# Token sums on VectorE, the first pair's rows by selection products, fillers among the gates, and a tail in permuted token order

## What is computed

```python
xn = layernorm(x)
# block 1: time mix (a scan over tokens, WKV) and channel mix
h = ln(xn); hp = shift(h); xk, xv, xr = mix(h, hp)
k, v, r = xk @ w_tk, xv @ w_tv, sigmoid(xr @ w_tr)
x1 = xn + r * wkv(time_decay, time_first, k, v)
h2 = ln(x1); x1 = x1 + sigmoid(cr @ w_cr) * (relu(ck @ w_ck) ** 2 @ w_cv)
# block 2: attention, 16 heads of 8 channels, weights = dense + gated low rank experts
pooled = xn.mean(axis=1)
gates, idx = softmax(top_k(relu(pooled @ gw1.T + gb1) @ gw2.T + gb2, 2))
q, k, v = svd_moe(xn, ...)            # per batch: Wm + sum of gated U S V
ctx = softmax(q @ k.T) @ v
out = x + x1 + svd_moe(ctx, ...)
```

## Time and profile before

| | |
|---|---|
| median of 3 runs | 487.45 us (486.83 to 490.58) |
| profiled execution | 487.07 us, span from first to last instruction 485.3 us |
| TensorE busy | 443.6 us, 91% |
| VectorE busy | 372.2 us, 77% |
| ScalarE busy | 354.2 us, 73% |
| POOL busy | 180.9 us, 37% |

### The profile page before, as it was taken

How to read it: one execution, slowest core, us unless ns; L and a number is a source line. 1 busy time by engine, 2 the same in 40 slices (tenths; PEclk the granted TensorE clock), 3 DMA queues, 4 the chain that set the end, 5 groups by cost and what they waited for, 6 DMA issues and landing times.

```text
span 485.3 us, 8374 instructions
## 1 busy us (share of the span) xinstructions
PE 443.6 (91%) x3156; PEld 147.9 (30%) x3158; DVE 372.2 (77%) x670; ACT 354.2 (73%) x453; POOL 180.9 (37%) x236
## 2 busy tenths in 40 slices
PE   2886998999999999999999999999999999989996
PEld 2751322222223322222232222222322222222275
DVE  7543997999988689999877899998778999940113
ACT  2266773689888666898986668989875689899651
POOL 7048940414651414146514141375141313751200
PEclk9999995999999999999999999999999999999998
DMA  6004421132323223323232232332322321102132
GB/s 219 11 8 52 61 23 23 12 54 26 57 22 59 19 45 33 51 28 56 23 58 22 28 51 50 30 52 26 57 24 22 55 45 12 28 9 80 31 105 91
DMA packets 46684, 21.35 MB, mean 44 GB/s; under 512 B 37556, under 2 KB 37684, under 8 KB 46644
## 3 DMA queue, kind: packets, MB, share of 16 engines
q1 hardware_dynamic: 45824, 20.13, 25.5%
q10 hardware_dynamic: 820, 0.68, 0.4%
HBM read 4.88 MB, written 5.24 MB: 21 GB/s over the span
## 4 chain that ended last, share of the span: by engine, by line
PE 58%; DVE 23%; ACT 13%; issue 2%; SPq 2%; DMA 1%; DVEq 0%
PE banks L1341 17%; DVE neg_half L1080 15%; PE banks L1330 12%; PE banks L1256 11%; ACT probs L887 9%; PE banks L1302 8%; DVE run L1038 3%; PE banks L1231 2%; PE banks L1164 2%; PE banks L1388 2%; PE banks L1383 2%; PE banks L1129 1%; ACT work L846 1%; SPq L431 1%; ACT work L844 1%
## 5 line engine op out<-in xcount | busy, mean ns | idle before, releaser
L1080 DVE TENSOR_REDUCE neg_half<-banks 128x1 f32<-128x512 f32 x512 | 319.1, 682 | 39.1 <-PE banks L1256 37.4
L887 ACT ACTIVATE probs<-banks 128x1024 f32<-128x1024 f32 x256 | 247.7, 1022 | 66.3 <-PE banks L1330 63.6
L1341 PE MATMUL banks<-probs,v_op 128*32 128x512 f32 x1024 | 137.2, 608 | 0.4 <-ACT probs L887 0.4
L1256 PE MATMUL banks<-k_main,q_main 64*128 64x512 bf16 x512 | 120.3, 388 | 15.0 <-DVE neg_half L1080 12.1
L1330 PE MATMUL banks<-q_main,k_main 64*128 64x512 bf16 x512 | 101.2, 382 | 5.0 <-ACT probs L887 3.7
L1330 PE MATMUL banks<-q_tail,k_tail 35*128 35x512 bf16 x512 | 100.9, 381 | 0.0
L1256 PEld LDWEIGHTS banks<-k_main,q_main 64*128 64x128 bf16 x512 | 36.0, 94 | 168.1 <-DVE neg_half L1080 145.2
L1330 PEld LDWEIGHTS banks<-q_main,k_main 64*128 64x128 bf16 x512 | 26.0, 95 | 44.5 <-ACT probs L887 32.1
L1330 PEld LDWEIGHTS banks<-q_tail,k_tail 35*128 35x128 bf16 x512 | 26.6, 95 | 23.7 <-issue 1.1
L1061 DVE TENSOR_TENSOR rec<-banks,quarter_in 128x512 f32<-128x512 f32 x4 | 2.8, 690 | 37.8 <-PE banks L1302 37.8
L700 POOL TENSOR_TENSOR work<-work 128x512 f32<-128x512 f32 x12 | 12.5, 1040 | 49.8 <-ACT work L872 49.8
(11 more groups left out here) (164 smaller groups left out, 429.4 us busy)
## 6 DMA issues: line engine op xcount, KB each, us to landing
ctx_dram<-ctx_sb SPq DMA_DIRECT2D x16, 256.0 KB, 2.0
q_main<-parts SPq DMA_DIRECT2D x64, 48.0 KB
k_main<-parts SPq DMA_DIRECT2D x64, 48.0 KB
parts<-ctx_dram SPq DMA_DIRECT2D x8, 256.0 KB, 4.4
mat_sb<-in_mats_dram SPq DMA_DIRECT2D x2, 768.0 KB, 5.3
q_tail<-max_parts SPq DMA_DIRECT2D x96, 2.0 KB
q_main<-parts SPq DMA_DIRECT2D x32, 32.0 KB
k_main<-parts SPq DMA_DIRECT2D x32, 32.0 KB
```

The costliest lines, as they stand in the source:

```text
L887: a.activation(probs[:, (2 * step + h) % 4, :, :], banks[:, 2 * h:2 * h + 2, :], ACT.Exp).then_inc(b_read, 1)
L1080: v.tensor_reduce(neg_half[:, s, u:u + 1], src, axis=AX.X, op=ALU.max, negate=True).then_inc(a_read, 1)
L1256: mm(dst, q_main[HALF * e:HALF * (e + 1), s, P * c:P * c + P], k_main[HALF * e:HALF * (e + 1), s, CHUNK * h:CHUNK * h + CHUNK], start=True ...
L1341: last = mm(banks[g:g + 32, PV_BANK, :], v_op[:, s % 2, step, e, :], probs[:, (2 * step + h) % 4, e, :], start=(step == 0), stop=(step == ...
```

## The change

1. Token sums: VectorE sums four tiles of a chunk (`sum_tiles`) into `xn_sum` once all tiles are normalised, and 4 products instead of 16 finish the sums. The transposes of x come before them.
2. The gate chain loses two steps (`chosen`, `gates`), and `warm(n)` issues n bf16 products of 128 columns into an unused bank: 4, 8, 32, 12 and 4 of them among the gate products.
3. Pair 0's rows: a selection matrix `row_of` (built by ScalarE in 22 small copies) times the parts gives `q_main` and `k_main` of pair 0, 12 products and 4 evictions. SyncE's `load_pair(0, 0)` is gone.
4. `turn_h`, the first `values_of` and `mix_product` move into the loop of places, by the table `FILL_JOBS` (place: jobs). ScalarE's order is as before, with two evictions of pair 0's rows ahead of `hT`.
5. `RT` and the last contexts (`ctx_out_T`) are written in permuted token order, so that the tail's weights are adjacent columns.
6. `k_tail` is set to 1.0 by one memset, and POOL adds the value bias in 4 instructions instead of 16.

```diff
+FILL_JOBS = {2: [("turn", 0), ("turn", 1)], 5: [("turn", 2), ("turn", 3)], 8: [("values", 0)], 11: [("values", 1)]}
+FILL_JOBS.update({14 + 2 * m: [("mixed", m)] for m in range(6)})
+FILL_JOBS.update({26: [("values", 2)], 28: [("values", 3)]})
+FILL_JOBS.update({29 + (m - 6): [("mixed", m)] for m in range(6, 12)})
+FILL_JOBS.update({35 + j: [("project", j, 1)] for j in range(4)})
+FILL_JOBS.update({39 + 4 * i + j: [("part", j, 1, i)] for i in range(2) for j in range(4)})
...
-            load_pair(0, 0)
             load_tails(0, 0)
...
-                for k in range(CHUNK // P):
-                    tc = 4 * (n % 2) + k
-                    here = V[:, 8 * (n // 2):8 * (n // 2) + 8, tc, :]
-                    last = g.tensor_tensor(here, here, vb_ob[:, 0:1, :].rearrange("p o (r w) -> p (o r) w", w=2 * HD),
-                                           ALU.add)
-                last.then_inc(v_ready, 1)
+                g.tensor_tensor(here, here, vb_ob[:, 0:1, :].rearrange("p o (r w) -> p r o w", w=2 * HD).to_broadcast(
+                    [P, 8, 4, 2 * HD]), ALU.add).then_inc(v_ready, 1)
...
+            act.wait_ge(rows_ps, 1)
+            a.copy(q_main[:, 0, 0:CHUNK], bank(0)).then_inc(q_rows_kept, 1)
+            act.wait_ge(rows_ps, 3)
+            a.copy(k_main[:, 0, CHUNK:], bank(3)).then_inc(k_rows_kept, 1)
...
+            def sum_tiles(n):
+
+                dve.wait_ge(xn_ready, 4 * n + 4)
+                v.tensor_reduce(xn_sum[:, n, :], xn_tok[:, 4 * n:4 * n + 4, :].rearrange("p k c -> p c k"), axis=AX.X,
+                                op=ALU.add).then_inc(xn_summed, 1)
...
+            for n in range(CHUNKS):
+                sum_tiles(n)
             dve.wait_ge(pooled_ps, B)
...
-            link(v.tensor_scalar(chosen[:, :], rank[:, :], 2.0, None, ALU.is_lt))
             dve.wait_ge(gexp_ready, 1)
-            link(v.tensor_tensor(gexp[:, :], gexp[:, :], chosen[:, :], ALU.mult))
+            link(v.scalar_tensor_tensor(gexp[:, :], rank[:, :], 2.0, gexp[:, :], ALU.is_lt, ALU.mult))
...
-            link(v.tensor_scalar(gates[:, :], gexp[:, :], gsum[:, 0:1], None, ALU.mult))
-            v.tensor_copy(gates_r[:, :, :], gates[:, :].rearrange("b (e o) -> b e o", o=1).to_broadcast(
-                [B, EXPERTS, RANK])).then_inc(gates_ready, 1)
+            v.tensor_scalar(gates_r[:, :, :], gexp[:, :].rearrange("b (e o) -> b e o", o=1).to_broadcast(
+                [B, EXPERTS, RANK]), gsum[:, 0:1], None, ALU.mult).then_inc(gates_ready, 1)
...
+            dve.wait_ge(rows_ps, 2)
+            v.tensor_copy(k_main[:, 0, 0:CHUNK], bank(2)).then_inc(k_rows_kept, 1)
+            dve.wait_ge(rows_ps, 4)
+            v.tensor_copy(q_main[:, 0, CHUNK:], bank(1)).then_inc(q_rows_kept, 1)
...
-                    v.tensor_tensor(RT[:, :, bass.ds(q * QT, QT)], x1[:, :, :], gx[:, :, :], ALU.add
-                    ).then_inc(rt_ready, 1)
+                    half, at = divmod(q, 2)
+                    there = RT[:, :, CHUNK * half:CHUNK * (half + 1)].rearrange("c b (k p) -> c b p k", k=CHUNK // P)
+                    there = there[:, :, QT // 4 * at:QT // 4 * (at + 1), :]
+                    for b in range(B):
+                        last = v.tensor_tensor(there[:, b, :, :], x1[:, b, :].rearrange("c (p k) -> c p k", k=CHUNK // P),
+                                               gx[:, b, :].rearrange("c (p k) -> c p k", k=CHUNK // P), ALU.add)
+                    last.then_inc(rt_ready, 1)
...
-                        v.tensor_tensor(ctx_T[:, n, :], ctx_T[:, n, :], den_T[:, n, :], ALU.mult
-                        ).then_inc(attn_ready, 1)
+                        v.tensor_tensor(ctx_out_T[n].rearrange("c (k p) -> c p k", k=CHUNK // P),
+                                        ctx_T[:, n, :].rearrange("c (p k) -> c p k", k=CHUNK // P),
+                                        den_T[:, n, :].rearrange("c (p k) -> c p k", k=CHUNK // P), ALU.mult
+                                        ).then_inc(attn_ready, 1)
...
+            def warm(times):
+
+                for _ in range(times):
+                    mm(bank(7)[:, 0:P], neg_ident[:, :], neg_ident[:, :], start=True, stop=True)
...
+            def pair_rows(j):
+
+                t, n = part_bank(j, 0)
+                pe.wait_ge(part_ready[j], PARTS)
+                for i in range(PARTS):
+                    last = mm(bank(j), row_of[:, t, i, :], parts[0:2 * HD, t, i, n, :], start=(i == 0),
+                              stop=(i == PARTS - 1))
+                last.then_inc(rows_ps, 1)
+
+            for j in (0, 2, 3, 1):
+                pair_rows(j)
...
-                        mm(bank(n)[:, P * k:P * k + P], token_tiles(columns_of(RT, n))[:, k, :], ident[:, :],
+                        mm(bank(n)[:, P * k:P * k + P], columns_of(RT, n)[:, P * k:P * k + P], ident[:, :],
...
-                        last = mm(bank(n)[:, P * k:P * k + P], token_tiles(ctx_T[:, n, :])[:, k, :],
+                        last = mm(bank(n)[:, P * k:P * k + P], ctx_out_T[n][:, P * k:P * k + P],
                                   w_eff[:, 3, n // 2, :], start=False, stop=(k == 3))
```

More of the change, by code:

```diff
@@ L99, in build @@
         gsum = sb("gsum", [B, 1])
-        gates = sb("gates", [B, EXPERTS])
         gates_r = sb("gates_r", [B, EXPERTS, RANK])
@@ L237, in build @@
         neg_ident_ok = sem("neg_ident_ok")
+        rows_cleared = sem("rows_cleared")
+        row_of_set = sem("row_of_set")
+        xn_summed = sem("xn_summed")
+        rows_ps = sem("rows_ps")
+        q_rows_kept = sem("q_rows_kept")
+        k_rows_kept = sem("k_rows_kept")
         ones_ok = sem("ones_ok")
@@ L279, in build @@
         mix_slot = [work[:, 1, n, :] for n in range(CHUNKS)]
+        ctx_out_T = [xnT[:, n // 2, CHUNK * (n % 2):CHUNK * (n % 2 + 1)] for n in range(CHUNKS)]
         mix_slot += [RT[:, n // 2, CHUNK * (n % 2):CHUNK * (n % 2 + 1)] for n in range(CHUNKS)]
@@ L557, in _ @@
             g.memset(q_tail[:, :, :], 0.0).then_inc(cleared, 1)
-            pool.wait_ge(cleared, 1)
-            pool.wait_ge(keys_cleared, 1)
-            for e in range(2):
-                ones = g.memset(k_tail[HALF * e + MAX_ROW:HALF * e + MAX_ROW + PARTS, :, :], 1.0)
-            ones.then_inc(ones_set, 1)
-            pool.wait_ge(ones_set, 1)
+            g.memset(row_of[:, :, :, :], 0.0).then_inc(rows_cleared, 1)
             g.memset(v_op[:, :, :, :, :], 0.0).then_inc(v_set, 1)
@@ L1125, in _ @@
             pe.wait_ge(ones_ok, 1)
-            for i in range(TILES):
-                b, k = divmod(i, TILES // B)
-                pe.wait_ge(xn_ready, i + 1)
-                last = mm(banks[:, 4, 24 + b:25 + b], xn_tok[:, i, :], ones_c[:, :], start=(k == 0),
-                          stop=(k == TILES // B - 1))
-                if k == TILES // B - 1:
-                    last.then_inc(pooled_ps, 1)
+            def warm(times):
+                for _ in range(times):
+                    mm(bank(7)[:, 0:P], neg_ident[:, :], neg_ident[:, :], start=True, stop=True)
             def turn_x(n):
@@ L1138, in turn_x @@
                 last.then_inc(x_transposed, 1)
+            for n in range(CHUNKS):
+                pe.wait_ge(xn_ready, 4 * n + 4)
+                turn_x(n)
+            for n in range(CHUNKS):
+                pe.wait_ge(xn_summed, n + 1)
+                last = mm(banks[:, 4, 24 + n // 2:25 + n // 2], xn_sum[:, n, :], ones_c[:, :], start=(n % 2 == 0),
+                          stop=(n % 2 == 1))
+                if n % 2 == 1:
+                    last.then_inc(pooled_ps, 1)
+            pe.wait_ge(neg_ident_ok, 1)
+            warm(4)
             pe.wait_ge(pooled_ready, 1)
@@ L1146, in _ @@
             ).then_inc(logits_ps, 1)
-            for n in range(1, CHUNKS):
-                turn_x(n)
+            warm(32)
             pe.wait_ge(gates_ready, 1)
@@ L1232, in mix_product @@
                    ).then_inc(kvr_ps, 1)
-            for u in range(CHUNKS):
-                turn_h(u)
-            values_of(0)
-            values_of(1)
-            for m in range(3):
-                mix_product(m)
+            pe.wait_ge(row_of_set, 22)
+            def pair_rows(j):
[7 more added lines that the diff above has]
+                pair_rows(j)
             pe.wait_ge(weff_ready, 4)
-            pe.wait_ge(ones_set, 1)
+            pe.wait_ge(keys_set, 1)
             def fill_place(it, pair, k, dst):
@@ L1253, in fill_place @@
                 e, c, h = place_of(k)
-                if k < 2:
-                    pe.wait_ge(main_in[s][e], (it + pair // SETS + 1) * 96)
+                n = it * SETS + pair
+                if n == 0 and k == 0:
+                    pe.wait_ge(q_rows_kept, 2)
+                    pe.wait_ge(k_rows_kept, 2)
+                elif n > 0 and k < 2:
+                    pe.wait_ge(main_in[s][e], (n // SETS + (s > 0)) * 96)
                 mm(dst, q_main[HALF * e:HALF * (e + 1), s, P * c:P * c + P],
@@ L1260, in between @@
             def between(n):
```

(30 more changed lines are left out.)

28 lines of the change are left out of this document (20 added, 8 removed).

## The result

| | median | profiled execution | span |
|---|---|---|---|
| before | 488.95 us (485.51 to 491.61, 20 runs) | 487.07 us | 485.3 us |
| changed | 486.23 us (484.42 to 488.56, 20 runs) | 488.56 us | 486.8 us |

The ratio is 0.9949, 95% interval 0.9928 to 0.9971: 0.5% faster, where 1.3% were forecast. Executions of one kernel differ by 4 us (changed) to 6 us (before).

What follows compares the result with a forecast made beforehand. The loop keeps TensorE busy 362.9 of 380.3 us, so gains must come from the opening or tail. 487.07 - 1.0 (opening) - 1.0 (clock at loop's start) + 0.3 (loop) - 4.2 (tail) = 481.2 us; range 475 to 485.5.

Steps and rivals of the forecast that it cites:

- Gate path: Opening up to the gates' product: sums +0.5, between gate products -0.5, two steps fewer -0.55, fillers +0.2; sum -0.3 us.
- Clock under the projections: Batch 0's projections: fillers hold TensorE's upper clock, about 1.0 us saved, last part written at 31.6.
- Pair 0's rows: Opening: products and evictions replace 12 DMAs, first score at 34.0 instead of 41.82 us, 7.8 to 10.7 earlier.
- Where the gain goes: Places before the loop: later mix chain eats most of the opening's gain, pair 0's scores at 75.7 us, -1.0.
- Clock at the loop's start: First scores to those of step 2: the lower clock may be avoided, 0 to -2.9 us, taken as -1.0.
- Loop: Addition into RT, split in two scattered halves: 0.1 us more in three quarters, +0.3; +1.7 if scattering doubles data time.
- Tail: After the loop: adjacent weights halve the RT products' time, the last context then sets the end; -4.6 to -3.4, taken -4.2 us.
- (1): Opening's gain arrives, only TensorE's own 34 us of products count: scores at 70, total 475 us; chance 0.10.
- (2): VectorE's scattered accesses cost twice: sums +1.6, RT +1.4, multiplication +0.4, total 484.6 us; chance 0.17.
- forecast mechanism: Whole kernel: the forecast's own account, range 479 to 483 us; chance 0.60.
- (3): Opening: clock falls while TensorE waits for the mix chain, 0.9 us more per job, 492 us from 15 jobs; chance 0.07.
- (4): Tail's gain absent: contexts land later because the first outputs' stores run beside them, total 485 us; chance 0.06.

Runs made afterwards that it cites:

- e1: Changed kernel with one line of ScalarE's order moved, scale_shift(0) ahead of keep_v(0) and keep_v(1): 481.99 us, ratio 0.9884 to the kernel before.
- e3: Changed kernel without its 60 filler products: 486.69 us, ratio 0.9969 to the kernel before.
- e4: Changed kernel with the strided token sums replaced by two contiguous additions a chunk: 484.79 us, ratio 0.9925 to the kernel before.
- e6: Kernel of e1 with 9 filler products behind each of the last three places, ahead of the loop: 482.95 us, ratio 0.9901 to the kernel before.
- e9: Kernel of e8 run once more, on one chip with two variants having fewer or no fillers: 479.46 us, ratio 0.9834 to the kernel before.
- e5: Kernel before with only pair 0's rows by selection products, FILL_JOBS, k_tail's memset and merged bias additions: 487.22 us, ratio 0.9988.
- e11: Kernel of e8 without any filler product: 478.87 us, ratio 0.9805 to the kernel before.
- e2: Kernel before with only the permuted order of RT and last contexts, giving adjacent weights in the tail: 486.19 us, ratio 0.9969.
- e7: Changed kernel with the scattered addition into RT moved from VectorE to POOL: 482.27 us, ratio 0.9894 to the kernel before.
- e8: Changed kernel with e1's ScalarE order, e4's contiguous sums and e7's RT addition on POOL together: 480.17 us, ratio 0.9834 to the kernel before.

## Why the prediction was wrong

The time, 486.23, lies outside the range (475 to 485.5). The direction was right. The step that failed is the opening: the first scores of pair 0 were to come 1.0 us earlier than before and came 4.05 later, because the mix chain started at 46.61 instead of 42.5. That its start decides was right (e1), its time was not.

Two things lie between the forecast of 481.2 and the time. The sum started from 487.07, and the 20 runs of the kernel before have a median of 488.95: 1.9 us of the difference are the base. And the gain was 2.7 us instead of 5.9. The profiled execution of the changed kernel lost 1.2 us to the clock under the rows' products and 2.7 at the loop's start, which e1's did not; without the two it would have taken 484.7 (an estimate from these rows), near the seven fastest of the 20 (484.42 to 485.02). In such an execution the terms are: opening +2.9 (forecast -1.0), loop's start -3.1 (-1.0), loop +1.0 (+0.3), tail -3.1 (-4.2), together -2.4 against the profile of before. Step by step:

**Gate path: -0.3 forecast, +1.1 measured.** Up to the first gate product +0.8 instead of +0.5: the sums were taken at the price of an unstrided reduction, 0.604, though the second rival had the doubled price, and took 0.95 each, +1.4; that part 6 would have the tiles ready 1.3 us earlier stood nowhere in the sum. The -0.5 between the gate products didn't come, only -0.1: eight fillers took 1.0 us there, as the transposes had; without them (e3) the two products are 0.6 apart. And the 32 fillers ran at 0.11 each, 3.5 us, against a chain of 2.4 us (0.6 shorter, as forecast): 1.05 late, not 0.2. The text had named 3.5 against 2.7 us and a delay of 0.8 as the bound, and taken a quarter of it.

**Clock under the projections: forecast -1.0, measured -1.6.** The halves ran at 0.46; first projection to last part 8.0 us instead of 9.6. The last part was written at 32.63, forecast 31.6, all by the gate path (1.4 late) and 0.2 behind it. That the fillers are the cause is shown in part: the seven profiles with 32 of them (changed kernel, e1, e4, e6 to e9) all have 3.9 us for the eight halves, and before, e3, e5 and e11 without them have 4.8 to 5.8, but e2, also without, has 3.92. And e3 and e11 show that fillers aren't worth it in sum.

**Pair 0's rows: 34.0 forecast, 36.59 measured.** Of the 2.6 us, 1.0 comes from above; behind the last part 4.0 us passed instead of 2.4. Of these 1.6, 1.2 are the clock: in e1, e4 and e5, where it held under the twelve products (2.76 us instead of 3.91), 2.8 us passed, and first places started at 35.56, 33.42 and 34.51.

**Where the gain goes: mechanism right, size short.** This is the step that failed by most. It said that the mix chain starts behind `values_of(1)`, is 19.3 us long, and leaves 1 of 7.8 to 10.7 us. Start forecast 42.5, measured 46.61; length 19.28; distance of the first projection from the last mix product 1.8, measured 1.81 (67.25 to 69.06). So the chain's length held, and its start was late by 4.1: 2.6 from the first place, 1.5 in the places up to 11, which I counted at VectorE's 0.604 alone although the four transpose groups, at the lower clock for a part, kept it waiting (idle 0.97 us ahead of place 3, and the first two groups took 1.97 us where the next two took 1.10). The scores of pair 0 came at 80.83, forecast 75.7: 4.1 by the start, and 1.0 more behind it, 0.7 up to mix product 11 and the rest behind the first projection, where a place and a projection were counted at 1.15 us and a round took up to 1.38. The forecast shared out the 1.38 us of a round as 2 x 0.23 for the places and 0.92 for the product; the rows in the section on the result show 0.32 for one place or two and 1.06 for the product. So the forecast counted a single place as half of two, and it costs as much as two.

**Clock at the loop's start: forecast -1.0, in the profile -0.4** (7.49 against 7.90). e1, e3, e4, e5, e6 and e11 have 4.77: when the clock holds, 2.7 us less than here and 3.1 less than before, near the 2.9 of the text. e6's fillers ahead of it did not end the slower runs, so the thin stretch is not shown to be their cause. In which executions the clock falls, and where, stays open. The executions of one kernel lie 2.5 to 6.9 us apart; the clock is a part of this, and the idle and the late contexts of e6 and e7 are others.

**Loop: forecast +0.3, measured +0.95** (three periods longer by 0.32). The scattered additions take 1.05 us for both halves against 0.69, the stride's price, not the instruction's fixed part: in e4 two contiguous additions of 256 columns take 0.7 together, as one of 512 does.

**Tail: forecast -4.2, measured -3.1.** The 32 `RT` halves run at 0.12, as forecast. The last multiplication takes 1.03 instead of 0.69, and the last eight halves 2.07 instead of 1.15, after 3.99 and 0.85 us of idle (the same count took 1.31 between the two), which is the lower clock's duration (granted clock 0.50 from 481.60 to 483.70). Both were named as bounds (0.4 and 0.8, together 1.2), and a third of them taken; both came whole.

**The rivals.** (1), the opening's gain arriving, did not happen, and e5 excludes it for this order. Its sum of 34 us for TensorE was too low: in e1 TensorE is busy for 38.9 us from the first place to the scores, so with these jobs at these places the scores can't come before 74.4. (2), scattered accesses at a higher price, is what happened beside the forecast mechanism: sums 1.6 times the unstrided price, additions and multiplication 1.5; its 484.6 lies near the time. I gave it 0.17 as if it excluded the forecast, while it is a surcharge that fits any case, and TensorE's strided loads spoke for it. (3), the clock falling while TensorE waits for the mix chain, did not happen in the changed kernel's profile, but it did in those of e3, e4 and e5; from the first addition to pair 0's scores e3 takes 35.8 us and the changed kernel 34.2, so it cost 1.6 there, far from what this rival needed. (4), contexts disturbed by the first stores: they landed 0.4 us sooner after their start than before in chunk 2 and 0.1 later in chunk 3, so no; only in e6's profile were they 0.9 later.

The Trainium skill's note on lines of 16 bytes (SBUF — State Buffer, Door 1), by which every access that goes to a new line pays a penalty, and on which rival 2 stood, agrees with VectorE's rows here, whose steps are 512 bytes: 0.95 against 0.604 us a sum, 1.03 against 0.69 a multiplication.

## What to carry to other kernels

When work is moved from ahead of a loop into it, look for the in-order engine that starts the longest chain behind it, and put that start first: here one line of ScalarE's order, kept as it was, cost 3 to 4 us (e1). Then add up what the moved work costs the busiest engine: what it gains at most is the time that this engine stood idle, here TensorE's 5.6 us between 31.85 and 44.73, and the rows' products took 2.8 to 3.9 of them. A surcharge that may hit every new instruction of a kind (a stride, a lower clock) belongs in the sum at its own chance, not in a rival of its own. And ask whether an instruction on the busiest engine can go to an idle one: `RT`'s addition on POOL brought 3 us in the loop (e8's profile), 0.7 a quarter even against the kernel before.

## What the runs showed of the hardware

- VectorE on fp32: reading or writing at steps of 512 bytes costs 1.5 to 1.6 times the unstrided duration (0.95 for 0.604, 1.05 for 0.69, 1.03 for 0.69 us). POOL took 1.43 us for the same scattered addition, and 1.28 for the contiguous one of 128x512 that stands right behind it (e7).
- Filler products of 128 columns in bf16 follow each other at 0.11 us at first (32 in 3.5), and at 0.07 in the places (9 in 0.6, e6).
- A bf16 product of 512 columns with 16 input rows fills its slot alone: 12 take 2.76 us at the upper clock (e4). Two products with 64 input rows each, one per head, go together in the same 0.22 us, as the scores at the loop's start do (76.26, 76.47 and 76.69 in e1), and two places take the 0.32 us of one (50.42 to 50.74, 62.73 to 63.04).
- While POOL fills a tile with a constant, VectorE's `TENSOR_SCALAR` from one fp32 tile in SBUF to another waits for the end of the fill: 1.16 and 1.05 us beside `k_tail` and `v_op` (before, at 7.13 and 8.28), 0.32 to 0.34 without a fill (changed kernel, at 7.03 to 7.78). The statistics' instructions are not held up (four in 0.84 to 0.87 us either way).
- 60 fillers bought no time: with 60, 40 and none the kernel took 479.5 to 480.2, 480.1 and 478.9 us.
